# Last stage of an audio tower on one Trainium2 core: transposes by DMA, and the mask and bias rows inside the transposed tile

## What is computed

```python
def ffn(x):                                   # x = layernorm(h), rows of 192
    logits = x @ router_w + router_b          # 4 experts
    idx = argmax(softmax(logits))             # top one
    h1 = gelu(x @ w1[e] + b1[e])              # every expert e, 192 hidden
    y = h1 @ w2[e] + b2[e]
    return y[idx] + x
h = h + ffn(layernorm(h))
```

## Times and profile before

| what | value |
|---|---|
| median of 3 runs | 2323.7 us |
| the profiled execution | 2322.24 us, span 2320.5 us |
| start of the last stage | about 1605 us |
| TensorE busy | 2162.2 us, 93% of the span |
| VectorE, ScalarE, GpSimd busy | 61%, 58%, 42% of the span |
| granted TensorE clock, mean | 0.974 |

### The profile page before, as it was taken

How to read it: one execution, slowest core, us unless ns; L and a number is a source line. 1 busy time by engine, 2 the same in 40 slices (tenths; PEclk the granted TensorE clock), 3 DMA queues, 4 the chain that set the end, 5 groups by cost and what they waited for, 6 DMA issues and landing times. The chain is left out here.

```text
span 2320.5 us, 60046 instructions
## 1 busy us (share of the span) xinstructions
PE 2162.2 (93%) x20736; PEld 1303.8 (56%) x20736; DVE 1419.9 (61%) x3727; ACT 1354.7 (58%) x3042; POOL 974.6 (42%) x1815
## 2 busy tenths in 40 slices
PE   5999999849999999999999999993999999999996
PEld 4999999714444444444444444441656655665563
DVE  4555555449999999999999999981222222222221
ACT  1333333328888888888888888882343344334331
POOL 1111111267777777777777777754111011101100
PEclk9999999959999999999999999996999999999998
DMA  5444344124444444444444444440000000000000
GB/s 147 122 110 133 109 122 122 55 39 88 86 89 87 86 87 88 86 87 87 87 87 87 87 87 87 87 74 4 15 19 18 18 19 18 18 19 18 18 18 20
DMA packets 443152, 158.63 MB, mean 68 GB/s; under 512 B 383456, under 2 KB 442475, under 8 KB 443115
## 3 DMA queue, kind: packets, MB, share of 16 engines
q1 hardware_dynamic: 443115, 158.15, 30.9%
HBM read 53.31 MB, written 12.48 MB: 28 GB/s over the span
## 5 line engine op out<-in xcount | busy, mean ns | idle before, releaser
L699 DVE TENSOR_REDUCE tops<-p_maxa 128x6 f32<-128x762 f32 x512 | 482.9, 943 | 83.1 <-PE p_maxa L542 83.0
L538 PE MATMUL p_s<-qm,kt 32*128 32x256 f16 x3072 | 433.3, 276 | 1.3 <-ACT probs L656 0.6
L613 PE MATMUL p_o<-probs,vn 127*32 127x256 f32 x6144 | 412.1, 386 | 0.2 <-DVE att L727 0.2
L654 ACT ACTIVATE probs<-p_s 128x512 f32<-128x512 f32 x512 | 305.7, 597 | 144.4 <-PE p_s L538 114.0
L940 ACT ACTIVATE gel<-f_w,b 128x512 f32<-128x512 f32 x192 | 131.9, 687 | 416.2 <-PE f_w L892 414.1
L701 DVE TENSOR_REDUCE tops<-p_maxb 128x4 f32<-128x508 f32 x512 | 345.8, 675 | 0.0
L1016 POOL TENSOR_TENSOR f_res<-h,f_hn 128x192 f32<-128x192 f32 x128 | 75.5, 590 | 584.1 <-DVE out_sb L989 426.9
L542 PE MATMUL p_maxa<-kt,qt 24*128 24x256 f16 (+1 forms) x2048 | 293.7, 250 | 24.0 <-issue 19.2
L538 PEld LDWEIGHTS p_s<-qm,kt 32*128 32x128 f16 x3072 | 163.3, 91 | 269.2 <-issue 112.7
L659 ACT ACTIVATE probs<-p_s 128x512 f32<-128x512 f32 x512 | 309.9, 605 | 0.0
L656 ACT ACTIVATE probs<-p_s 128x512 f32<-128x512 f32 x512 | 303.3, 592 | 0.0
(11 more groups left out here) (185 smaller groups left out, 4397.0 us busy)
## 6 DMA issues: line engine op xcount, KB each, us to landing
xn<-in_xn SPq DMA_DIRECT2D x32, 768.0 KB, 6.3
xt_a<-in_xt SPq DMA_DIRECT2D x32, 512.0 KB, 4.3
out<-out_sb SPq DMA_DIRECT2D x32, 381.0 KB
xt_b<-in_xt SPq DMA_DIRECT2D x32, 256.0 KB, 5.2
xt<-hx SPq DMA_TRANSPOSE x128, 2.4
kt<-qk SPq DMA_TRANSPOSE x128, 2.8
qt<-qk SPq DMA_TRANSPOSE x128, 2.4
qm<-qk SPq DMA_TRANSPOSE x128, 2.8
```

Of the source, the lines that this page charges most:

```text
L538: return nc.tensor.matmul(o, kt[full(j), r, kind, g, :], qm[full(j), r % 2, versions, g, :], start=True, stop=True, skip_group_check=True)
L613: last = nc.tensor.matmul(p_o[32 * j:32 * j + 32, blocks, :], vn[0:NP, r, src:src + 32], probs[0:NP, r % 2, QUAD * g + j, kind * 256:(kind ...
L654: nc.scalar.activation(probs[:, r % 2, h:h + 2, 512:768], p_s5[:, :, :].rearrange("p (h x) n -> p h (x n)", h=2), ACT.Exp, scale=SCALE).th ...
L699: nc.vector.tensor_reduce(top[:, q, pair, 4:10], p_ma[:, 0:6, 0:NP], AX.X, ALU.max, negate=True).then_inc(dve_ma[u], 1)
```

## The change

- The four fp32 transposes a group through PE and PSUM, their copies and the transposes of the picks are gone. POOL makes the high fp16 part of x, the low part, the residual and a packed tile `pk`, and SP issues two DMA transposes per group: `xt` (12 tiles of 128 x 128, from `hx`, 1536 columns of fp16: high and low parts of four blocks) and `pkt` (4 tiles, from `pk`, 512 columns).
- `pk` holds for each token 64 columns of the high part, the mask (columns 64 to 67) and the choice for the bias (68 to 71 and 96 to 99). The fifth product of a chunk runs over `pkt` with the low part of the weights and the mask's table in one 128-row operand, so the sixth product is gone. The bias is one product of 128 rows a block in place of two with 8 rows. FAR is 2^15 in both operands in place of 2^60 in one.
- The second layer is still one fp32 product a chunk and block, but goes chunk by chunk: `down(c)` runs over the four blocks, and follows `up(c + 2)`. The last two chunks, `down(i - 1, 4)` and `down(i - 1, 5)`, stand in the next body, behind `up(i, 0)` and the router, and behind `up(i, 1)`. The finished blocks of group i - 1 and their store therefore belong to body i. PSUM holds three tiles `f_w` and four `f_y`; `gel` has three chunks in place of six.
- x is normalized two groups ahead, once per block (192 columns) in place of twice (192 and 64).
- SP's order in body i: store of group i - 1, transpose `pkt` of group i + 1, transpose `xt` of group i + 2, each behind its waits.
- `setup` loads and casts a third part of w1 and of the router's weights, and a 128-row b2; the table `far` is made there. `ident16` is gone. VectorE clears `pk` (128 x 2048 fp16) at the start of the last stage.

The diff, cut to its core:

```diff
-FAR = 2.0 ** 60
+FAR = 2.0 ** 15
...
-        p_y = [ps(f"f_y{i}", [128, 512]) for i in range(2)]
+        p_y = [ps(f"f_y{i}", [128, 512]) for i in range(G)]
...
+            for i in range(-2, 3):
+                body(i, i % U, (i - 1) // 2)
+            rounds = (NG - 5) // U
+            with eng.Fori(0, rounds) as j:
+                for r in range(U):
+                    body(j * U + (3 + r), (3 + r) % U, j * 2 + (2 + r) // 2)
+            for i in range(3 + U * rounds, NG + 1):
+                body(i, i % U, (i - 1) // 2)
+        @block.sync
+        def _(sp):
+            def ready(signal, count):
+                sp.wait_ge(signal, count)
+                sp.sem_inc(sp_ready, 1)
+            def body(i, r, half):
+                if within(i - 1, NG):
+                    ready(dve_y, seen(i * G))
+                    dst = dram["out"][bass.ds(i - 1, 1), :, :, :].rearrange("g b p d -> p (g b) d")
+                    sp.dma_start(dst, out_sb[0:NP, (r - 1) % 2, :, :]).then_inc(stored[(r - 1) % 2], 16)
+                if within(i + 1, NG):
+                    ready(dve_pick, seen(i + 2))
+                    ready(pool_x, seen((i + 2) * G))
+                    if within(i - 1, NG):
+                        ready(pe_w[HCH - 1], seen(i))
+                        ready(pe_w2[0], seen(i))
+                    sp.dma_start_transpose(pkt[:, (r + 1) % 2], pk[:, (r + 1) % U].rearrange("p g n -> p (g n)")).then_inc(dma_pk, 16)
+                if within(i + 2, NG):
+                    ready(pool_x, seen((i + 3) * G))
+                    if within(i - 2, NG):
+                        ready(pe_w[HCH - 1], seen(i - 1))
+                    sp.dma_start_transpose(xt[:, (r + 2) % U].rearrange("p g k n -> p (g k) n"),
+                                           hx[:, r % 2].rearrange("p g n -> p (g n)")).then_inc(dma_x, 16)
+            loop(sp, body)
+            for par in range(2):
+                sp.wait_ge(stored[par], 16 * ((NG + 1 - par) // 2))
...
-                nc.tensor.transpose(p_t[k % 2][:, 0, :], hn[:, k % 2, 0:128], t.ident[:, :])
-                nc.tensor.transpose(p_t[k % 2][:, 1, :], hn[:, k % 2, 128:256], t.ident[:, :]).then_inc(pe_t, 1)
...
-                        nc.tensor.matmul(o, far[:, c * 128:(c + 1) * 128], pick_t[:, par].rearrange("p g n -> p (g n)"),
-                                         start=False, stop=True).then_inc(pe_w[c], 1)
...
+            (wa, wal, wb, wbl), wc = t.split["w1"], t.third["w1"]
+            (ra, ral, rb, rbl), rc = t.split["wrouter"], t.third["wrouter"]
+            def router(i, r):
+                if within(i + 1, NG):
+                    pe.wait_ge(dma_x, seen(16 * (i + 2)))
+                    pe.wait_ge(steps[0], seen(i + 1))
+                    for k in range(G):
+                        x = xt[:, (r + 1) % U, k]
+                        o = p_log[:, k, :]
+                        nc.tensor.matmul(o, x[:, 0, :], ra[:, :], start=True, stop=False)
+                        nc.tensor.matmul(o, x[:, 0, :], ral[:, :], start=False, stop=False)
+                        nc.tensor.matmul(o, x[:, 1, :], rb[:, :], start=False, stop=False)
+                        nc.tensor.matmul(o, x[:, 1, :], rbl[:, :], start=False, stop=False)
+                        last = nc.tensor.matmul(o, x[:, 2, :], rc[:, :], start=False, stop=True)
+                    last.then_inc(pe_log, 1)
+            def up(i, r, c):
+                if within(i, NG):
+                    if c == 0:
+                        pe.wait_ge(dma_x, seen(16 * (i + 1)))
+                        pe.wait_ge(dma_pk, seen(16 * (i + 1)))
+                    if c >= 3:
+                        pe.wait_ge(act_g[c - 3], seen(i + 1))
+                    else:
+                        pe.wait_ge(act_g[c + 3], seen(i))
+                    cols = slice(c * 128, (c + 1) * 128)
+                    x, o = xt[:, r], p_w[c % 3][:, :]
+                    nc.tensor.matmul(o, wa[:, cols], x[:, :, 0, :], start=True, stop=False)
+                    nc.tensor.matmul(o, wal[:, cols], x[:, :, 0, :], start=False, stop=False)
+                    nc.tensor.matmul(o, wb[:, cols], x[:, :, 1, :], start=False, stop=False)
+                    nc.tensor.matmul(o, wc[:, cols], x[:, :, 2, :], start=False, stop=False)
+                    nc.tensor.matmul(o, wbl[:, cols], pkt[:, r % 2], start=False, stop=True).then_inc(pe_w[c], 1)
+            def down(g, ring, c):
+                if within(g, NG):
+                    pe.wait_ge(act_g[c], seen(g + 1))
+                    for k in range(G):
+                        o, n = p_y[k][:, 0:C], slice(k * 128, (k + 1) * 128)
+                        if c == 0:
+                            pe.wait_ge(dve_y, seen((g - 1) * G + k + 1))
+                            nc.tensor.matmul(o, pkt[:, ring, k, :], t.b2[:, :], start=True, stop=False)
+                        last = nc.tensor.matmul(o, gel[:, c % 3, n], t.w2[:, c, :], start=False, stop=(c == HCH - 1))
+                        if c == HCH - 1:
+                            last.then_inc(pe_y, 1)
+                    if c < HCH - 1:
+                        last.then_inc(pe_w2[c], 1)
+            def body(i, r, half):
                 for c in range(HCH):
+                    up(i, r, c)
+                    if c == 0:
+                        router(i, r)
+                    if c < 2:
+                        down(i - 1, (r - 1) % 2, c + HCH - 2)
+                    else:
+                        down(i, r % 2, c - 2)
...
+                n = (i + 2) * G + k
+                if within(i + 2, NG):
+                    act.wait_ge(pool_x, seen(n - 1))
+                    nc.scalar.activation(hn[:, k % 2, :], t.h[:, bass.ds(n * C, C)], ACT.Identity,
+                                         scale=t.rstd[:, bass.ds(n, 1)], bias=t.shift[:, bass.ds(n, 1)]).then_inc(act_ln, 1)
+            def body(i, r, half):
                 for c in range(HCH):
                     if c < G:
                         norm(i, c)
                     if within(i, NG):
                         act.wait_ge(pe_w[c], seen(i + 1))
+                        if c >= 3:
+                            act.wait_ge(pe_w2[c - 3], seen(i + 1))
+                        elif c < 2:
+                            act.wait_ge(pe_w2[c + 3], seen(i))
+                        else:
+                            act.wait_ge(pe_y, seen(i * G))
+                        nc.scalar.activation(gel[:, c % 3, :], p_w[c % 3][:, :], ACT.Gelu, bias=t.b1[:, c:c + 1]).then_inc(act_g[c], 1)
...
+                if within(i - 3, NG):
+                    dve.wait_ge(dma_pk, seen(16 * (i - 2)))
...
+            def output(i, r, half, k):
+                if within(i - 1, NG):
+                    n = (i - 1) * G + k
+                    dve.wait_ge(pe_y, seen(n + 1))
+                    dve.wait_ge(pool_x, seen(n + 1))
...
+            nc.gpsimd.memset(one[:, :], 1.0).then_inc(consts, 1)
+            pool.wait_ge(consts, 2)
+            def body(i, r, half):
+                if not within(i + 2, NG):
+                    return
                 for k in range(G):
+                    n = (i + 2) * G + k
+                    ring = (r + 2) % U
+                    x = hx[:, r % 2, k, :]
+                    pool.wait_ge(act_ln, seen(n + 1))
+                    if k == 0 and within(i, NG):
+                        pool.wait_ge(dma_x, seen(16 * (i + 1)))
+                    if k == 0 and within(i - 2, NG):
+                        pool.wait_ge(dma_pk, seen(16 * (i - 1)))
+                        pool.wait_ge(dve_y, seen((i - 1) * G))
+                    nc.gpsimd.tensor_tensor(x[:, 0:C], hn[:, k % 2, :], one[:, :].broadcast_to([128, C]), ALU.mult).then_inc(pool_hi, 1)
+                    nc.gpsimd.tensor_tensor(res[:, ring, k, :], t.h[:, bass.ds(n * C, C)], hn[:, k % 2, :], ALU.add)
+                    nc.gpsimd.tensor_tensor(pk[:, ring, k, 0:CB], hn[:, k % 2, CA:C], one[:, :].broadcast_to([128, CB]), ALU.mult)
+                    pool.wait_ge(pool_hi, seen(n + 1))
+                    nc.gpsimd.tensor_tensor(x[:, C:2 * C], hn[:, k % 2, :], x[:, 0:C], ALU.subtract).then_inc(pool_x, 1)
```

More of the change, by code:

```diff
@@ L795, in feed_forward @@
         sem = lambda name: ctx.enter_context(nc.semaphore(name))
[L796 to L800, removed]
+        hn = sb("f_hn", [128, 2, C])
+        hx = sb("f_hx", [128, 2, G, 2 * C], F16)
+        xt = sb("f_xt", [128, U, G, 3, 128], F16)
+        res = sb("f_res", [128, U, G, C])
+        pk = sb("f_pk", [128, U, G, 128], F16)
+        pkt = sb("f_pkt", [128, 2, G, 128], F16)
         logit = sb("logit", [128, G, NE])
@@ L850, in router @@
[L850 to L870, removed]
@@ new lines, in choose @@
+                nc.vector.tensor_scalar(pk[:, (r + 1) % U, :, 64:68], pk[:, (r + 1) % U, :, 68:72], -1.0, FAR, ALU.add, ALU.mult)\
+                    .then_inc(dve_pick, 1)
+            def output(i, r, half, k):
[3 more added lines that the diff above has]
```

(30 more changed lines are left out.)

220 lines of the change are left out of this document (56 added, 164 removed).

## The result

The changed kernel takes **2514.4 us** (median of 4 runs, 2511.69 to 2521.22) against 2323.2 us: ratio 1.083, 95% interval [1.0804, 1.0855]. The forecast was 2551 us, 2485 to 2620. The profiled execution has a span of 2511.0 us.

The account below looks back on a forecast made before the run. PE's order of work was taken as the bound before (21.3 us a group). After the change, a 26.5 us loop plus 2.2 for the clock gives 28.7; 29 such loops with entry, tail, setup and launch give 2551 us, range 2485 to 2620.

Parts of the forecast that it names:

- The bound before and the one busy engine: Last stage before: PE's work is the bound, 21.3 us a group; each store keeps one DMA engine of 16 busy, hidden.
- PE by itself: PE's own work in the changed last stage: 18.3 us a group in place of 21.3.
- Added: PE's new work a group: four full-height bias products, 1.5 us, and five more fp16/fp32 type changes, 1.0 us.
- rival A: Last stage: transposes do not wait for the store, PE's 18.3 us are the period; 2236 us, 3.8% faster; chance 0.07.
- The order of the queue: SP's queue: `pkt` of group i + 1 waits for the whole store in front of it on the store's one engine.
- The loop: Last stage: `pkt` landing, PE's products, additions, store, next `pkt` follow in strict order: 26.5 us, 28.7 with the clock.
- landing to store, full clock: From `pkt` landing to store issue: PE's up, router, down, up, down 6.0 us plus additions 0.9, together 6.9 us.
- clock: PE's clock falls while it stands in each loop; 5 us at the lower level add 2.2 us.
- store issued to next landing: Store on one engine 19.0 us, then `pkt`'s part 0.5 and 0.1 added to PE: 19.6 us.
- period: Time of one group in the changed last stage: 28.7 us against 21.3 before.
- Rival C: SP cannot hand over a transpose during a store: 2 to 3 us a loop more, 2610 to 2640; chance 0.06 plus 0.02.
- Rival B: Transposes share the store's engine without PE waiting its turn: engine bound, 20.4 us a group, 2304 us; chance 0.04.

Follow-up runs that it names:

- e6: Kernel before, its 8-row operands (mask table, picks, high and low bias) padded with zero rows to 128: 2277.7 us, ratio 0.980.
- e1: Changed kernel with each group's store cut in two DMAs, 112 and 15 partitions, in place of one of 127: 2123.1 us, ratio 0.914.
- e2: Kernel before with its stores cut in two DMAs, 112 and 15 partitions: 2306.7 us, ratio 0.993.
- e4: Changed kernel whose store writes only 61 of the 127 rows of each block, still on one engine: 2203.7 us, ratio 0.949.
- e5: Changed kernel whose stores are issued by ScalarE on its own DMA queue, the transposes staying on SP's: 2243.6 us, ratio 0.965.
- e10: Changed kernel with 47 filler products a body in the time in which TensorE waits for the transpose: 2466.9 us, ratio 1.062.
- e8: Changed kernel with the last two second-layer chunks of group i - 1 put before `up(i, 0)` on TensorE: 2449.8 us, ratio 1.054.
- e3: Changed kernel with SP issuing the store last in a body, behind both transposes: 2259.2 us, ratio 0.973.
- e9: Changed kernel with e8's TensorE order and VectorE's additions also put before the choice: 2259.5 us, ratio 0.972.
- e7: Changed kernel with 38 filler products behind each body, in the time in which TensorE waits: 2508.9 us, ratio 1.080.

## Why the prediction was right

**The bound before and the one busy engine**: right, by e6 (less work on TensorE, less time) and by e1 and e2. **PE by itself**: the forecast had 18.3 us a group, and 15.3 is what TensorE takes alone (e1). (Its list of removed and added parts would even give 21.3 - 4.8 + 2.5 = 19.0; the 18.3 are its second sum.) The step that failed is "Added", the changes of type: 1.5 us for the bias products, where about 0.45 is measured, and 1.5 us for each of six `down`, where 1.3 is (2002.25 to 2003.55 in the changed kernel). The price was read in the earlier trace rows between L906 and L907, a step from 128 rows to 8 and from fp32 to fp16 at once; by e6 it belongs to the rows, and the change removes every 8-row operand. The rest is six `up` at 1.2, read from a pitch that also ends in an 8-row product; without one it is 1.08 (2001.17 to 2002.25). 1.05 + 1.2 + 0.7 make up the 3.0. This did not decide the time, since TensorE is not the bound, but it made rival A 113 us too slow: 2236 where e1 has 2123, of which some 15 are e1's shorter last store.

**The order of the queue**: right. `f_pkt` lands 19.1 us after its issue, and with the store on another queue 5.5 us. That the transposes wait for the store in front of them is shown by e1, e4 and e5. Of the two sections of the Trainium skill that stood beside it, in DMA: Bandwidth & Descriptors, both agree with the runs: order within a queue under Queues, rings and completion order (e5 against the changed kernel), and the engines used by 127 partitions against 112 and 15 under Why a DMA increments its semaphore by 16 and not by 1 (19 us against 2.7).

**The loop**, term by term:

| term | forecast | measured |
|---|---|---|
| landing to store, full clock | 6.9 | 6.35 (mean of e10) |
| clock | 2.2 | 1.6 (7.96 less 6.35) |
| store issued to next landing | 19.6 | 19.8 (mean; 19.88 in the turn shown) |
| period | 28.7 | 27.7 |

The 6.9 were too long for the same reason as above: two `down` at 1.5 in place of 1.3, two `up` at 1.2 in place of 1.08. The clock's 2.2 had 5 us at the lower level; the trace has some 3.3 us in most turns and up to 6.6 in others. The assumption that the router keeps its pace holds: its 20 products take 0.58 us at the lower level (1998.90 to 1999.48) and 0.52 at the full one (2007.11 to 2007.63 in e10). TensorE stands 10.3 to 10.6 us a turn and not the forecast's 7 to 9, because its own work is 3 us shorter. 29 loops at 1.0 us less are 28 of the 37 us between forecast and measurement; body 1 began 3 us earlier than forecast, its own loop took 25.8 in place of 26.5, and the end and the launch make up the rest.

**Rival C** was half right, and my reason against it wrong. SP does stand, 15.3 us in the instruction for `f_pkt`, as the rival said. But it gets free at 2020.20, some 3 us before the store's end (2004.36 + 0.22 + 18.8 = 2023.4 by the earlier trace rows), `f_pkt` still lands within 1 us of that end, and the 2.8 us of SP's instruction for `f_xt` fit in. SP's standing is also not the whole wait: behind its instruction `f_pkt` takes another 3.8 us to land (19.1 less 15.3), in e1 only 1.4 (2.6 less 1.2). By e8 the forecast's list of links was too short: I named TensorE's path from landing to store, and not VectorE's beside it, which alone gives 25.7. **Rival B**'s bound, the engine's load, is what e3 and e9 have when the loop is open: 19.1 and 19.3 us and not its 20.4, since the transposes' share of 2.1 us is 1.5 and there are no gaps.

## What to carry to other kernels

Before a transfer is added to a queue, look at what stands in front of it there, engine by engine: the mean DMA share of 0.07 was here one engine of 16 that is busy all the time, with the whole store of 127 partitions on it. Then ask whether that store waits for the transfer behind it; if so the two add up in each turn, and cutting the store in two (112 + 15 partitions), giving it a queue of its own, putting it behind the transposes, or making it wait for nothing new each took the loop away here (2123, 2244, 2259 and 2260 us against 2514). When an order is changed to open a loop, list every engine on which the released work is queued.

## What I had not expected of the hardware

- SP's instruction for a 512-column transpose takes 15.3 us behind a 127-partition store, 1.2 us without (e5).
- The clock fell also after only 2.6 to 2.9 us without products, in 26 of 29 loops of e7, and even after 1.5 to 1.9 us in 7 of 29 of e4; with 0.7 to 1.0 us of standing (e10) every loop was fast. A fall cost 1.2 us (7.55 less 6.38) where the clock was down for some 3.3 us of a turn, and 2.8 us (9.19 less 6.35) where it was down for 6.6.
- A product with 8 rows between products with 128 costs 0.2 us more than one padded with zeros (0.31 + 0.32 less 2 x 0.216 for L892); padding made the kernel before 2.0% faster (interval 1.8 to 2.1%).
